# Expert stage: the down products as three split passes with the token rows moving

## The chip, the cores and the metric

One core of one Trainium2 chip runs the whole program. The metric is the device time of that core in microseconds (us); a run is one launch of the program, and the median of three runs is given. A profile is one more execution, with every instruction's start and duration. Engines: PE is TensorE (with PEld for its weight loads), DVE is VectorE, ACT is ScalarE, POOL is GpSimd, SP is SyncE.

## What is computed

Eight layers run one after the other on x of 128 x 64 tokens with 128 channels: four cross attentions with a feed-forward layer behind each. The change touches the third feed-forward layer alone, a mixture of 32 experts (64 hidden units each) and one shared expert (128 hidden units). From the reference:

```python
logits = jnp.einsum('th,eh->te', x, gate_w)
scores = jax.nn.sigmoid(logits)
...                                   # two of four groups of experts, then the best 8 of 32
topk_w = topk_w / (topk_w.sum(-1, keepdims=True) + 1e-20)
topk_w = topk_w * ROUTED_SCALING
...
g = jnp.einsum('th,eih->eti', x, expert_gate)
u = jnp.einsum('th,eih->eti', x, expert_up)
outs = jnp.einsum('eti,ehi->eth', jax.nn.silu(g) * u, expert_down)
...
final = (gathered * topk_w[:, :, None]).sum(1)
shared = _mlp(residuals, shared_gate, shared_up, shared_down)
return final.reshape(orig_shape) + shared
```

x goes in normalised, and the result is added to x times a gate. All is float32.

## The kernel before, and how its expert stage is built

The stage is the function `experts`. The 8192 tokens are 16 groups of 512 (4 tiles of 128). The hidden units of all experts are computed for every token, side by side: 2048 routed ones and 128 shared ones, cut into 17 **blocks** of 128 units (NB = 17, of which NR = 16 are routed). A block holds two experts. One block of one group, called m = 17 g + j, goes through the engines so:

- PE, `gate_up`: two products of weights (standing) with the group's 512 token columns (moving), each as three passes of `product3` (L354, L355, L356). An operand is split beforehand into a high and a low part of type fp32r, and high x high, high x low and low x high are summed in PSUM. So six matmuls of 512 columns. `ps_g` and `ps_u` have two PSUM banks each, so `gate_up` of block m waits for the multiplication of block m - 2 (`u_read`).
- ACT, `silu` (L1615): silu of the gate product, from PSUM.
- DVE, `mult` (L1662): silu times the up product (which is in PSUM) into `aT`, which has two buffers.
- DVE, `weight` (L1672): `aT` times the routing weights of the block's two experts, `wb`, both in SBUF. Block 16 is the shared expert and has none; there a tiny memset signals instead. `wb` is a row of the weights spread over 64 partitions by DMAs that SP issues (L1526), into a ring of 8 buffers (WR = 8).
- PE, `down` (L1581): four float32 matmuls with the 128 x 128 pieces of `aT` standing and the down weights moving, summed over the 17 blocks in one PSUM bank, `acc`. The trace shows each as two instructions.

At a group's end DVE adds `acc` times the gate to x (`added`, L1779), and the next group's first `down` waits for that. Between the blocks of group g the work for group g + 1 is placed by the number j in `body`: on PE the transposes of the normalised rows (j = 0), the router (j = 1), the turn of the weights (j = 11); on ACT the matching copies and the exponential of the router's sigmoid, which needs another activation table than silu; on DVE the split of hT (L343, L347; j = 1), 13 parts of routing arithmetic (two in each of j = 2 to 7, one in j = 8), the moments of group g + 2 (L302, L307; j = 9) and its scaling (L316, four instructions; j = 11). POOL does two small operations on 4 columns per group for the normalisation (L324, L326) and nothing else. Each engine runs its own list in the order of the code; `by_pairs` makes a loop over pairs of groups and writes the last pair out. In iteration j PE does `gate_up` of block j + 2, then `down` of block j; ACT does `silu` of j + 2, DVE `mult` and `weight` of j + 2, then the extra work of j.

Of the kernel before, what the change touches and what calls it, by code (L numbers as in the profile page):

```python
# [36 lines left out]
class Chip:  # L37
# [1432 lines left out]

def experts(c, d):


# [2 lines left out]
    V, A, T, G = nc.vector, nc.scalar, nc.tensor, nc.gpsimd  # L1478
    n = c.ngroup
    NB, NR = W2N // P, NE2 * I2 // P  # L1480
    WR = 8
    w = c.carve()
    hn = w([TG, P])
    hT = [w([GT]), w([GT])]
    r = c.carve(c.parts)
    hTh, hTl = [r([GT]), r([GT])], [r([GT]), r([GT])]
    wgh, wgl, wuh, wul = (r([W2N]) for _ in range(4))
    sg, aT = [w([GT]), w([GT])], [w([GT]), w([GT])]
    wT, wb = [w([GT]), w([GT])], [w([GT]) for _ in range(WR)]
    wts = [w([TG, NE2]), w([TG, NE2])]  # L1490
# [1 line left out]
    top, gt, eq = w([TG * 4, 8]), w([TG, 4, 4]), w([TG, 4, 4])  # L1492
    gs, rank, t8, ws = w([TG, 4]), w([TG, 4]), w([TG, 8]), w([TG])
    ps_g, ps_u = (tuple(c.ps[:, i + j, :] for j in range(2)) for i in (0, 2))
    acc, ps_x = c.ps[:, 6, :], c.ps[:, 7, :]
    norm = Norm(c, "f2_ln", hn)
    sem = lambda s: c.sem("f2_" + s)
    x_ready, x_out, gu_ready, silu_ready, u_read, a_ready, y_ready, added, link = (
        sem(s) for s in ("x", "x_out", "gu", "silu", "u_read", "a", "y", "added", "link"))
    down_done, wts_ready, norm_link = sem("down"), sem("wts"), sem("norm_link")  # L1500
    high_ready, low_ready, w_high, w_low = sem("high"), sem("low"), sem("w_high"), sem("w_low")
# [4 lines left out]
    def ahead(g, u, j, k=2):  # L1506

        return (g, u, j + k) if j + k < NB else (g + 1, 1 - u, j + k - NB)

    def at(g, u, j):  # L1510

# [2 lines left out]
    with nc.Block() as block:  # L1514
        @block.sync
        def _(sp):
            def spread(g, u):

                sp.wait_ge(x_out, g * 3 + 3)
                sp.dma_start(rows[u], wT[u][0:NE2, :]).then_inc(rows_in, 16)  # L1520
                sp.wait_ge(rows_in, g * 16 + 16)
                for j in range(NR):
                    if not (isinstance(g, int) and g == 0 and j < WR):
                        sp.wait_ge(a_ready, g * NB + (j - WR + 1) if j >= WR else g * NB + (j - WR))
                    for e in range(2):
# [9 lines left out]
            by_pairs(sp, n, body)  # L1535

        @block.gpsimd
        def _(pool):
            with pool.Fori(0, n) as g:
                norm.pool(pool, g)  # L1540

        @block.tensor
        def _(te):
# [45 lines left out]
            turn_weights(0, 0)  # L1589

            def body(g, u, last_pair):
# [12 lines left out]
            by_pairs(te, n, body)  # L1604

        @block.scalar
        def _(act):
# [19 lines left out]
            act.sem_inc(added, 1)  # L1627
# [3 lines left out]
            take_hT(0, 0), sigmoid_exp(0), silu(0, 0, 0), silu(0, 0, 1), take_weights(0, 0)  # L1631

            def body(g, u, last_pair):
                end = last_pair and u == 1
                for j in range(NB):
                    if not (end and j + 2 >= NB):
# [8 lines left out]
            by_pairs(act, n, body)  # L1645

        @block.vector
        def _(ve):
# [5 lines left out]
            def mult(g, u, j):  # L1654
                m, b = at(g, u, j)
                ve.wait_ge(silu_ready, m + 1)
                if not (isinstance(g, int) and g == 0 and j < 2):
                    if j < 2:
                        ve.wait_ge(y_ready, g) if j == 1 else ve.wait_ge(down_done, g * (NB - 1))
                    else:  # L1660
                        ve.wait_ge(down_done, g * (NB - 1) + (j - 1))
                out = V.tensor_tensor(aT[b], sg[b], ps_u[b], ALU.mult)  # L1662
                out.then_inc(u_read, 1)
                if j == NB - 1:
                    ve.wait_ge(u_read, m + 1)
                    V.memset(c.pause[:, 1:2], 0.0).then_inc(a_ready, 1)
# [96 lines left out]
            def body(g, u, last_pair):  # L1763
                end = last_pair and u == 1
                for j in range(NB):
                    if not (end and j + 2 >= NB):
                        block_of(*ahead(g, u, j))
                    if j == 1 and not end:
                        split(g + 1, 1 - u)
                    if 2 <= j < 9 and not end:  # L1770
# [3 lines left out]
                        norm.take_moments(ve, g + 2)  # L1774
                    if j == 11 and not last_pair:
                        norm.scale(ve, g + 2)
                ve.wait_ge(y_ready, g + 1)
# [4 lines left out]
            by_pairs(ve, n, body)  # L1782

# [398 lines left out]
def program(nc, d, layers=range(8)):  # L2182

    ctx = ExitStack()
    with ctx:
# [13 lines left out]
        c.close_work()  # L2199
        for layer in layers:  # L2200

            parts = {0: 4 * GT + 12 * P * 2 + 32 * D, 1: 4 * GT + 2 * NE0 * QKV, 2: 4 * GT + 12 * P * 2 + 32 * D, 5: 4 * GT + 4 * W2N, 6: 4 * GT + 12 * P * 2 + 64 * D}
            c.open_work({0: 17 * 1024, 2: 17 * 1024, 6: 13 * 1024, 1: 12 * 1024, 5: 12 * 1024}.get(layer, 26 * 1024), parts.get(layer, 0))
            if layer in (0, 2, 6):
                wide_attention(c, d, layer // 2)
            elif layer == 4:
# [95 lines left out]
```

## Time and profile before

| what | value |
| --- | --- |
| median of 3 runs | 3582.87 us (3581.49 to 3583.41) |
| profiled execution, own time | 3580.62 us |
| its span | 3578.5 us |
| mean granted TensorE clock | 0.959 of full speed |
| PE busy | 90% |
| DVE busy | 71% |
| ACT busy | 46% |
| POOL busy | 33% |
| expert stage | about 1929 to 2619 us of the span |
| its period per group | 41.5 us |

The profile has a page for the whole span and views on request: timelines of single instructions, groups of equal instructions by line, waits (who waited for whom), and windows with each engine's busy time. The period per group comes from line L1779, which runs once per group, from 1995.3 to 2617.8 us with 15 periods between. "Busy" says nothing of the gaps between instructions, some tens of ns each.

### The profile page before, as it was taken

The page shows a single profiled execution, that of the slowest core. Times are in us where ns is not written, and L with a number is a line of the kernel's source. Part 1 is how long each engine was busy: PE and PEld are TensorE (multiplying, and loading weights), DVE is VectorE, ACT ScalarE, POOL GpSimd, SP SyncE. Part 2 cuts the span into 40 slices and gives each one's busy share as a digit, 9 for nine tenths or more (in the row PEclk, how much of TensorE's full clock was granted, in tenths as well). Part 3 has the DMA queues.
Part 4 walks back from the last instruction along what each step waited for, and adds up shares of the span by engine and source line. Part 5 has one row for each costly group of instructions (what it writes and reads, how often), then busy time and mean ns, then how long its engine had stood idle before and what let it go on. Part 6 is the DMA issues. An engine that isn't in the chain of part 4 may idle for free. (4 is left out here: it accounts for less than half of the span.)

```text
span 3578.5 us, 78637 instructions
## 1 busy us (share of the span) xinstructions
PE 3205.1 (90%) x27370; PEld 2479.6 (69%) x27370; DVE 2528.8 (71%) x7156; ACT 1630.0 (46%) x3136; POOL 1170.3 (33%) x1359
## 2 busy tenths in 40 slices
PE   5999888888888999948997999999989999999978
PEld 3666577777777666645666888888866666666646
DVE  3666688888887555557777777777767777777732
ACT  2566433333333656516665333333245555555533
POOL 3555300000001555443441000000036566566532
PEclk9999989999999999958998999999999999999989
DMA  4000000000000000001111323333300000000001
GB/s 143 10 9 9 1 1 1 1 1 1 1 1 3 10 9 9 3 0 57 26 25 43 105 95 96 107 108 103 104 21 8 9 9 7 9 7 9 5 15 32
DMA packets 70603, 108.15 MB, mean 30 GB/s; under 512 B 13984, under 2 KB 24224, under 8 KB 69952
## 3 DMA queue, kind: packets, MB, share of 16 engines
q1 hardware_dynamic: 66048, 96.89, 8.7%
q10 hardware_dynamic: 4416, 9.59, 0.9%
q8 instruction: 65, 1.06, 0.1%
q14 instruction: 74, 0.61, 0.1%
HBM read 97.51 MB, written 5.24 MB: 29 GB/s over the span
## 5 line engine op out<-in xcount | busy, mean ns | idle before, releaser
L354 PE MATMUL ps<-parts 96*128 96x512 f32 (+2 forms) x2080 | 884.1, 425 | 22.0 <-DVE work L1662 7.4
L356 PE MATMUL ps<-parts 96*128 96x512 f32 (+2 forms) x2080 | 799.6, 384 | 0.0
L355 PE MATMUL ps<-parts 96*128 96x512 f32 (+2 forms) x2080 | 799.5, 384 | 0.0
L354 PEld LDWEIGHTS ps<-parts 96*128 96x128 f32 (+1 forms) x2080 | 402.5, 193 | 120.9 <-issue 47.1
L739 ACT ACTIVATE work<-ps 128x512 f32<-128x512 f32 x512 | 305.8, 597 | 394.5 <-PE ps L356 367.7
L324 POOL TENSOR_TENSOR rstd<-mv,eps 128x4 f32<-128x4 f32 x144 | 29.9, 208 | 1348.3 <-DVE mv L307 1348.2
L356 PEld LDWEIGHTS ps<-parts 96*128 96x128 f32 (+1 forms) x2080 | 400.3, 192 | 66.9
L355 PEld LDWEIGHTS ps<-parts 96*128 96x128 f32 (+1 forms) x2080 | 403.9, 194 | 44.7
L1615 ACT ACTIVATE work<-ps 128x512 f32<-128x512 f32 x272 | 163.0, 599 | 453.5 <-PE ps L356 453.4
L702 PEld LDWEIGHTS ps<-work 64*64 64x64 f32 x8192 | 221.6, 132 | 207.8 <-issue 207.8
L2095 DVE SCALAR_TENSOR_TENSOR work<-ps,work 128x192 f32<-128x192 f32 x896 | 323.8, 410 | 54.2 <-PE ps L356 41.9
L848 DVE TENSOR_REDUCE work<-work 128x8 f32<-128x512 f32 (+1 forms) x256 | 175.7, 686 | 231.9 <-ACT work L751 231.6
L523 POOL TENSOR_TENSOR work<-work 128x512 f32<-128x512 f32 x256 | 266.8, 1042 | 149.9 <-DVE work L850 148.4
L1581 PEld LDWEIGHTS ps<-early,work 128*128 128x128 f32 x2176 | 281.3, 191 | 29.7 <-DVE work L1672 11.3
L1581 PE MATMUL ps<-early,work 128*128 128x128 f32 x2176 | 289.0, 276 | 8.1 <-DVE x L1779 8.0
L702 PE MATMUL ps<-work 64*64 64x128 f32 x8192 | 282.6, 275 | 11.6 <-ACT work L792 11.6
L1662 DVE TENSOR_TENSOR work<-work,ps 128x512 f32<-128x512 f32 x272 | 185.8, 683 | 133.3 <-PE ps L1581 133.1
L832 DVE SCALAR_TENSOR_TENSOR ps<-ps,work 128x512 f32<-128x512 f32 x192 | 134.1, 698 | 135.7 <-PE ps L625 127.6
L835 DVE TENSOR_REDUCE work<-ps 128x8 f32<-128x512 f32 x256 | 176.9, 691 | 64.2 <-PE ps L625 57.6
L316 DVE TENSOR_SCALAR work<-x,mv,rstd 128x128 f32 (+1 forms) x456 | 174.7, 446 | 50.8 <-POOL rstd L326 50.8
L792 ACT ACTIVATE work<-ps 128x512 f32<-128x512 f32 x256 | 152.9, 597 | 112.1 <-PE ps L675 112.1
L1672 DVE TENSOR_TENSOR work<-work 128x512 f32<-128x512 f32 x256 | 177.1, 692 | 15.5 <-DMA work<-expert_rows 2.9
(283 smaller groups left out, 5700.4 us busy)
## 6 DMA issues: line engine op xcount, KB each, us to landing
work<-expert_rows SPq DMA_DIRECT2D x512, 128.0 KB, 2.9
work<-in_ctxT SPq DMA_DIRECT2D x72, 192.0 KB, 2.3
out<-x SPq DMA_DIRECT2D x16, 256.0 KB, 2.3
work<-work SPq DMA_DIRECT2D x224, 16.0 KB
early<-in_l0f_w ACTq DMA_DIRECT2D x1, 1536.0 KB, 15.3
early<-in_l2f_g SPq DMA_DIRECT2D x1, 1088.0 KB, 6.6
early<-in_l2f_u SPq DMA_DIRECT2D x1, 1088.0 KB, 8.8
early<-in_l2f_d SPq DMA_DIRECT2D x1, 1088.0 KB, 11.0
```

What stands on the lines that cost most here:

```text
L354: T.matmul(out, lh, rh, start=True, stop=False)
L355: T.matmul(out, lh, rl, start=False, stop=False)
L356: return T.matmul(out, ll, rh, start=False, stop=True)
L523: G.tensor_tensor(pn[t % 2], pr[t % 2][:, :, 0:S], bc(rec[t % 2], 2, S), ALU.mult).then_inc(p_ready, 1)
L702: pv = T.matmul(acc[p][half, t, :], ptT[t % 2][rows, j, half], vp[t % 2][rows, int(p != b), j, :], start=(un.p == 0 and j == 0 and (t == 0 ...
L739: A.activation(vp[t % 2][:, e, :, :].rearrange("p j c -> p (j c)"), ps_v[e], ACT.Copy).then_inc(v_done[e], 1)
L835: V.tensor_reduce(mx[t % 2], ps_s, AX.X, ALU.max).then_inc(max_ready, 1)
L848: V.tensor_reduce(den[t % 2], pr[t % 2], AX.X, ALU.add).then_inc(sum_ready, 1)
L1581: last = T.matmul(acc[:, t * D:(t + 1) * D], aT[b][:, t * P:(t + 1) * P], c.w["l2f_d"][:, j, :], start=(j == 0 and t == 0), stop=(j == NB ...
L1662: out = V.tensor_tensor(aT[b], sg[b], ps_u[b], ALU.mult)
L1672: V.tensor_tensor(aT[b], aT[b], wb[j % WR], ALU.mult).then_inc(a_ready, 1)
L2095: V.scalar_tensor_tensor(out=part_sum[t % 2][e], in0=z, scalar=r, in1=part_sum[t % 2][e], op0=ALU.mult, op1=ALU.add).then_inc(z_read, 1)
```

## The change

The down product gets the same form as gate and up: its weights `wd` stand, and the 512 token columns of `aT` move, in three passes of fp32r parts. The weights are split once at the start of the stage (high part by ACT, low part by POOL). `aT` is split in every block: ACT copies the high part to `ah` (`high_part`), POOL subtracts it from `aT` into `al` (`low_part`), both in rings of three (AR = 3); PE's `down` waits for `al_ready`. The second buffer of `aT` is freed by POOL's subtraction now: `mult` of block m waits for `al_ready` of block m - 2. The sum comes out with channels on the partitions, in one of two PSUM banks `ps_d`; ACT copies it to SBUF (`take_down`, `yT`) and PE turns it back with four transposes into `acc` (`turn_back`), three blocks into the next group; DVE adds it there (`add`, j = 3). `gate_up` and `silu` run three blocks ahead of `down` where they ran two; DVE stays at two. The ring `wb` shrinks from 8 to 4 buffers. The first pair of groups is now written out as well.

```diff
-    WR = 8
+    WR, AR = 4, 3
...
+    ps_d = tuple(c.ps[:, 4 + i, :] for i in range(2))
...
+            def low_part(g, u, j):
+
+                m, b = at(g, u, j)
+                pool.wait_ge(ah_ready, m + 1)
+                if not (isinstance(g, int) and g == 0 and j < AR):
+                    pool.wait_ge(down_done, downs_before(g, j))
+                pool.sem_inc(low_begun, 1)
+                G.tensor_tensor(al[j % AR], aT[b], ah[j % AR].bitcast(FP), ALU.subtract).then_inc(al_ready, 1)
+
+            norm.pool(pool, 0)
+            pool.wait_ge(wd_high, 1)
+            G.tensor_tensor(wdl.rearrange("p j c -> p (j c)"), c.w["l2f_d"].rearrange("p j c -> p (j c)"),
+                            wdh.bitcast(FP).rearrange("p j c -> p (j c)"), ALU.subtract).then_inc(wd_low, 1)
+            norm.pool(pool, 1)
+
+            def body(g, u, last_pair):
+                for j in range(NB):
+                    low_part(g, u, j)
+                    if j == 10 and not last_pair:
+                        norm.pool(pool, g + 2)
...
             def down(g, u, j):
                 m, b = at(g, u, j)
-                te.wait_ge(a_ready, m + 1)
+                te.wait_ge(al_ready, m + 1)
                 if j == 0:
-                    te.wait_ge(added, g + 1)
+                    need(te, yt_out, g - 1)
+                T.matmul(ps_d[u], wdh[:, j, :], ah[j % AR], start=(j == 0), stop=False)
+                T.matmul(ps_d[u], wdl[:, j, :], ah[j % AR], start=False, stop=False)
+                T.matmul(ps_d[u], wdh[:, j, :], al[j % AR], start=False, stop=(j == NB - 1)).then_inc(down_done, 1)
+
+            def turn_back(g):
+
+                te.wait_ge(yt_out, g + 1)
+                need(te, added, g)
                 for t in range(TG):
-                    last = T.matmul(acc[:, t * D:(t + 1) * D], aT[b][:, t * P:(t + 1) * P], c.w["l2f_d"][:, j, :],
-                                    start=(j == 0 and t == 0), stop=(j == NB - 1), skip_group_check=True)
-                last.then_inc(y_ready if j == NB - 1 else down_done, 1)
+                    last = T.transpose(acc[:, t * P:(t + 1) * P], yT[:, t * P:(t + 1) * P], c.w["ident"][:, :])
+                last.then_inc(y_ready, 1)
...
+            def high_part(g, u, j):
+
+                m, b = at(g, u, j)
+                act.wait_ge(a_ready, m + 1)
+                if not (isinstance(g, int) and g == 0 and j < AR):
+                    act.wait_ge(down_done, downs_before(g, j))
+                A.activation(ah[j % AR], aT[b], ACT.Copy).then_inc(ah_ready, 1)
+
+            def take_down(g, u):
+                act.wait_ge(down_done, g * NB + NB)
+                need(act, y_ready, g)
+                A.activation(yT, ps_d[u], ACT.Copy).then_inc(yt_out, 1)
...
-                    if not (end and j + 2 >= NB):
+                    if not (end and j + 1 >= NB):
+                        high_part(*ahead(g, u, j, 1))
+                    if not (end and j + LAG >= NB):
                         silu(*ahead(g, u, j))
+                    if j == 1 and not (isinstance(g, int) and g == 0):
+                        take_down(g - 1, 1 - u)
...
                 ve.wait_ge(silu_ready, m + 1)
                 if not (isinstance(g, int) and g == 0 and j < 2):
-                    if j < 2:
-                        ve.wait_ge(y_ready, g) if j == 1 else ve.wait_ge(down_done, g * (NB - 1))
-                    else:
-                        ve.wait_ge(down_done, g * (NB - 1) + (j - 1))
+                    ve.wait_ge(al_ready, m - 1)
                 out = V.tensor_tensor(aT[b], sg[b], ps_u[b], ALU.mult)
...
+                    if j == 3 and not (isinstance(g, int) and g == 0):
+                        add(g - 1)
```

**POOL's list**, before, for the whole stage (a loop of two instructions per group, L324 and L326 in `norm.pool`):

```order
L1539 UNCONDITIONAL_BRANCH
L1539 ISA
L324 TENSOR_TENSOR rstd<-mv,eps 128x4
L326 TENSOR_TENSOR rstd<-rstd,half 128x4
L1539 REGISTER_ALU
L1539 COMPARE_AND_BRANCH
```

And of the change, the stage's start with the first two groups (L1575 the low part of the down weights, L1571 `low_part`):

```order
L324 TENSOR_TENSOR rstd<-mv,eps 128x4
L326 TENSOR_TENSOR rstd<-rstd,half 128x4
L1575 TENSOR_TENSOR parts<-early,parts 128x2176
L324 TENSOR_TENSOR rstd<-mv,eps 128x4
L326 TENSOR_TENSOR rstd<-rstd,half 128x4
L1571 TENSOR_TENSOR parts<-work,parts 128x512 x11
L324 TENSOR_TENSOR rstd<-mv,eps 128x4
L326 TENSOR_TENSOR rstd<-rstd,half 128x4
L1571 TENSOR_TENSOR parts<-work,parts 128x512 x17
```

POOL now has 17 subtractions of 512 columns per group, and the normalisation's two operations stand behind the eleventh of them.

**DVE's list** in the loop, before, at a group's end (L1662 `mult`, L1672 `weight`, L1779 the addition to x):

```order
L1662 TENSOR_TENSOR work<-work,ps 128x512
L1672 TENSOR_TENSOR work<-work 128x512
L1779 ISA
L1779 SCALAR_TENSOR_TENSOR x<-ps,tg,x 128x512
L1656 REGISTER_ALU
L1662 TENSOR_TENSOR work<-work,ps 128x512
```

And of the change, in iteration j = 3, behind `mult` and `weight` of block 5 (L1766 to L1775 routing parts 2 and 3, L1856 the addition, L1735 `mult` of block 6):

```order
L1763 REGISTER_ALU
L1764 MEMSET pause 1x1
L1766 MAX work<-work 128x8 x16
L1728 REGISTER_ALU
L1769 TENSOR_TENSOR work<-work 128x16
L1772 REGISTER_ALU
L1774 TENSOR_TENSOR work<-work 128x64
L1775 TENSOR_TENSOR work<-work 128x64
L1856 ISA
L1856 SCALAR_TENSOR_TENSOR x<-ps,tg,x 128x512
L1732 REGISTER_ALU
L1735 TENSOR_TENSOR work<-work,ps 128x512
```

The addition moved from a gap between groups to the iteration with the longest routing part.

## Rows read from the trace of the kernel before

**Rows 1.** The page, part 1: busy time, share of the span, instructions.

```profile
PE 3205.1 (90%) x27370; PEld 2479.6 (69%) x27370; DVE 2528.8 (71%) x7156; ACT 1630.0 (46%) x3136; POOL 1170.3 (33%) x1359
```

**Rows 2.** Window of one group: PE, PEld, DVE, ACT, POOL busy; PEclk; DMA.

```profile
2037.50:2079.00 41.50, 40.72 (x253) 35.84 (x252) 32.20 (x99) 13.70 (x22) 1.21 (x2) 1.00 0.32 103
```

**Rows 3.** Waits, 1995 to 2500 us: us in total, times, longest.

```profile
ACT work L1615 <- PE ps L356: 336.0, 193, 2.4
DVE work L1662 <- PE ps L1581: 94.9, 84, 1.8
...
PEld ps L354 <- DVE work L1662: 7.5, 24, 0.5
PE ps L1581 <- DVE x L1779: 6.6, 13, 0.5
```

**Rows 4.** Timeline of one block: start us, us, engine, line, operation.

```profile
2103.04 0.48 PE L354 MATMUL ps<-parts 128*128 128x512 f32 x1
...
2103.35 0.40 PE L355 MATMUL ps<-parts 128*128 128x512 f32 x1
...
2104.49 1.05 PE L1581 MATMUL ps<-early,work 128*128 128x128 f32 x8
...
2105.30 0.48 PE L354 MATMUL ps<-parts 128*128 128x512 f32 x1
```

**Rows 5.** Groups by form, 2000 to 2500 us: busy us, mean ns, idle before.

```profile
L1662 DVE TENSOR_TENSOR work<-work,ps 128x512 f32<-128x512 f32 x203 | 138.6, 683 | 93.7 <-PE ps L1581 93.5
L1672 DVE TENSOR_TENSOR work<-work 128x512 f32<-128x512 f32 x191 | 132.2, 692 | 9.9 <-DVE work L1662 0.6
L1615 ACT ACTIVATE work<-ps 128x512 f32<-128x512 f32 x203 | 121.6, 599 | 332.1 <-PE ps L356 331.9
...
L1615 ACT ACT_TABLE_LOAD x12 | 15.4, 1283 | 0.2
...
L316 DVE TENSOR_SCALAR work<-x,mv,rstd 128x128 f32 x48 | 13.3, 341 | 0.0
...
L302 DVE BATCH_NORM_STATS2 st<-x 128x6 f32 x48 | 10.4, 279 | 0.0
...
L347 DVE TENSOR_TENSOR parts<-work,parts 128x512 fp32r<-128x512 f32 x12 | 8.3, 692 | 0.4
```

**Rows 6.** Timeline, start of the stage.

```profile
1928.78 2.02 ACT L1629 ACTIVATE parts<-early 128x2176 fp32r<-128x2176 f32 x1 [2.37 <-PEq L2217]
...
1938.20 0.22 DVE L1683 TENSOR_SCALAR work<-work 128x128 f32<-128x128 f32 x1
...
1938.99 0.63 PE L355 MATMUL ps<-parts 128*128 128x512 f32 x1
...
1939.42 0.63 PE L356 MATMUL ps<-parts 128*128 128x512 f32 x1
...
1945.80 0.29 DVE L1743 TENSOR_TENSOR work<-work 128x128 f32<-128x128 f32 x1
```

**Rows 7.** By line, whole span: duration ns min/median/max.

```profile
L505 POOL TENSOR_TENSOR parts<-work,parts x58: 1285/1304/1316, 80.9 to 3365.5; 96x512 fp32r<-96x512 f32 x58
L840 DVE TENSOR_TENSOR work<-work x128: 166/169/1209, 2640.7 to 3408.5; 128x8 f32<-128x8 f32 x128
L843 DVE TENSOR_TENSOR work<-ps,work x256: 678/688/692, 67.5 to 3408.8; 128x512 f32<-128x512 f32 x128
L513 POOL TENSOR_TENSOR parts<-parts,zero x128: 1260/1279/1327, 55.3 to 3378.6; 96x512 fp32r<-96x512 f32 x128
```

**Rows 8.** Timeline of the wide-head attention, POOL and DVE.

```profile
2677.91 1.29 POOL L503 TENSOR_TENSOR parts<-work,zero 96x512 fp32r<-96x512 f32 x1
2678.02 1.21 DVE L840 TENSOR_TENSOR work<-work 128x8 f32<-128x8 f32 x1
```

**Rows 9.** Window of the gated stage; columns as in rows 2.

```profile
600.00:800.00 200.00, 166.91 (x1036) 151.89 (x1036) 162.85 (x556) 62.35 (x185) 10.95 (x21) 0.91 0.00 1
```

More of the change, by code:

```diff
@@ L1469, in _, with by_two_groups, both @@
             by_pairs(ve, n, body)
+def by_two_groups(eng, n, body):
+    def both(it, last):
+        for u in range(2):
+            body(it * 2 + u, u, last)
+    by_twos(eng, n // 2, both)
 def experts(c, d):
@@ L1487, in experts @@
     wgh, wgl, wuh, wul = (r([W2N]) for _ in range(4))
+    wdh, wdl = (r([NB, D]) for _ in range(2))
+    ah, al = [r([GT]) for _ in range(AR)], [r([GT]) for _ in range(AR)]
+    yT = w([GT])
     sg, aT = [w([GT]), w([GT])], [w([GT]), w([GT])]
@@ L1500, in experts @@
     down_done, wts_ready, norm_link = sem("down"), sem("wts"), sem("norm_link")
+    low_begun = sem("low_begun")
+    ah_ready, al_ready, yt_ready, yt_out, wd_high, wd_low = (sem(s) for s in ("ah", "al", "yt", "yt_out", "wd_high", "wd_low"))
+    LAG = 3
     high_ready, low_ready, w_high, w_low = sem("high"), sem("low"), sem("w_high"), sem("w_low")
@@ L1504, in experts, with ahead, behind, downs_before @@
     LINKS = 16
-    def ahead(g, u, j, k=2):
+    def ahead(g, u, j, k=LAG):
         return (g, u, j + k) if j + k < NB else (g + 1, 1 - u, j + k - NB)
+    def behind(g, u, j, k):
+        return (g, u, j - k) if j >= k else (g - 1, 1 - u, j - k + NB)
+    def downs_before(g, j):
+        last = j - AR if j >= AR else {0: NB - 2, 1: NB - 1, 2: NB - 3}[j] - NB
+        return g * NB + last + 1
     def at(g, u, j):
@@ L1533, in body @@
                     spread(g + 1, 1 - u)
-            by_pairs(sp, n, body)
+            by_two_groups(sp, n, body)
         @block.gpsimd
         def _(pool):
-            with pool.Fori(0, n) as g:
-                norm.pool(pool, g)
+            def low_part(g, u, j):
[15 more added lines that the diff above has]
+                        norm.pool(pool, g + 2)
+            by_two_groups(pool, n, body)
         @block.tensor
@@ L1589, in _ @@
             turn_weights(0, 0)
+            gate_up(0, 0, 2)
+            te.wait_ge(wd_low, 1)
             def body(g, u, last_pair):
@@ L1602, in body @@
                     down(g, u, j)
-            by_pairs(te, n, body)
+                    if j == 2 and not (isinstance(g, int) and g == 0):
+                        turn_back(g - 1)
+            by_two_groups(te, n, body)
+            turn_back(n - 1)
         @block.scalar
@@ L1630, in _ @@
             A.activation(wuh, c.w["l2f_u"], ACT.Copy).then_inc(w_high, 1)
-            take_hT(0, 0), sigmoid_exp(0), silu(0, 0, 0), silu(0, 0, 1), take_weights(0, 0)
+            take_hT(0, 0), sigmoid_exp(0)
+            A.activation(wdh.rearrange("p j c -> p (j c)"), c.w["l2f_d"].rearrange("p j c -> p (j c)"), ACT.Copy).then_inc(wd_high, 1)
+            silu(0, 0, 0), silu(0, 0, 1), take_weights(0, 0), high_part(0, 0, 0), silu(0, 0, 2)
             def body(g, u, last_pair):
@@ L1635, in body @@
                 for j in range(NB):
-                    if not (end and j + 2 >= NB):
+                    if not (end and j + 1 >= NB):
+                        high_part(*ahead(g, u, j, 1))
+                    if not (end and j + LAG >= NB):
                         silu(*ahead(g, u, j))
+                    if j == 1 and not (isinstance(g, int) and g == 0):
+                        take_down(g - 1, 1 - u)
                     if j == 0 and not end:
@@ L1643, in body @@
                         take_weights(g + 1, 1 - u)
-            by_pairs(act, n, body)
+            by_two_groups(act, n, body)
+            take_down(n - 1, 1)
         @block.vector
@@ L1766, in body @@
                     if not (end and j + 2 >= NB):
-                        block_of(*ahead(g, u, j))
+                        block_of(*ahead(g, u, j, 2))
                     if j == 1 and not end:
@@ L1776, in body, with add @@
                         norm.scale(ve, g + 2)
+                    if j == 3 and not (isinstance(g, int) and g == 0):
+                        add(g - 1)
+            def add(g):
                 ve.wait_ge(y_ready, g + 1)
@@ L1780, in body @@
                                        op0=ALU.mult, op1=ALU.add).then_inc(added, 1)
-            by_pairs(ve, n, body)
+            by_two_groups(ve, n, body)
+            add(n - 1)
 def gated_attention(c, d):
@@ L2200, in program @@
         for layer in layers:
-            parts = {0: 4 * GT + 12 * P * 2 + 32 * D, 1: 4 * GT + 2 * NE0 * QKV, 2: 4 * GT + 12 * P * 2 + 32 * D, 5: 4 * GT + 4 * W2N, 6: 4 * GT + 12 * P * 2 + 64 * D}
-            c.open_work({0: 17 * 1024, 2: 17 * 1024, 6: 13 * 1024, 1: 12 * 1024, 5: 12 * 1024}.get(layer, 26 * 1024), parts.get(layer, 0))
+            parts = {0: 4 * GT + 12 * P * 2 + 32 * D, 1: 4 * GT + 2 * NE0 * QKV, 2: 4 * GT + 12 * P * 2 + 32 * D, 5: 10 * GT + 6 * W2N, 6: 4 * GT + 12 * P * 2 + 64 * D}
+            c.open_work({0: 17 * 1024, 2: 17 * 1024, 6: 13 * 1024, 1: 12 * 1024, 5: 8704}.get(layer, 26 * 1024), parts.get(layer, 0))
             if layer in (0, 2, 6):
```

1 line of the change is left out of this document (removed).

## The prediction

> **What bounds the kernel now.** I read the page's busy shares first: PE is busy 90% of the span, DVE 71% [rows 1]. The change touches one stage, so the next view is a window of one group there: of 41.5 us PE is busy 40.72, DVE 32.20, ACT 13.70, POOL 1.21, with the clock granted in full [rows 2]. The waits say who waits for whom [rows 3]: ACT and DVE wait for PE (336.0 and 94.9 us of 500), while PE waits for DVE 7.5 us at a gate product and 6.6 us at a down product, the latter once per group at the addition to x. So PE sets the pace. But DVE is close behind. Its 99 instructions have 30 to 40 ns between them (`mult` of 0.683 us and `weight` of 0.692 us [rows 5] take about 0.71 and 0.70 us of its list each), so it is occupied 32.2 + 99 x 0.035 = 35.7 us of the 41.5.
>
> **PE: what is removed and added.** A block takes 2105.30 - 2103.04 = 2.26 us [rows 4]. The five gate and up passes from 2103.35 to 2104.49 are 0.228 us apart, and the down product takes the 0.81 us from there, plus some 0.08 that the first pass behind it loses (0.31 us to the second one, not 0.228). With nine passes a block is 9 x 0.228 = 2.05 us: 0.21 us less. Per group that is 17 x 0.21 = 3.6 us; the wait for the addition, 6.6 / 13 = 0.5 us, goes too; the four transposes of `turn_back` cost 0.5 us. PE alone would need 17 x 2.05 = 34.9 us for blocks and about 2.3 us for transposes, router and turns: 37.2 us per group. If PE stayed the bound, 41.5 - 37.2 = 4.3 us per group would be gained.
>
> **DVE: not less work, and a new neighbour.** DVE's 35.7 us stay, so it has only 1.5 us per group to spare against 37.2, 0.09 us per block. What the change adds beside it is POOL's subtraction, 17 times per group. Its duration is that of L505, the same operation with the same kinds of operands on 96 partitions: 1.30 us [rows 7]. What such an operation does to DVE the attention stages show. L840 reads two SBUF tensors of 8 columns and takes 0.169 us at the median, but up to 1.209 us [rows 7]. In the timeline it starts at 2678.02, 0.11 us behind a POOL operation that runs from 2677.91 to 2679.20, and ends at 2679.23 [rows 8]. So it waited for POOL's operation to within about 0.15 us of its end, a hold of about 1.15 us. L843, of the same kind but with one operand in PSUM, never exceeds 0.692 us in 256 instances [rows 7]. Hence `mult` (one operand in PSUM) can run beside the subtraction; `weight`, `split`'s L347 and the TENSOR_TENSOR parts of the routing can't start during it.
>
> The Trainium skill ("SBUF — State Buffer", section "SBUF: two separate sides") states this as a rule: DVE and GpSimd share one pair of SBUF ports, as an exclusive lock for a whole instruction, and a DVE instruction takes it with two SBUF inputs or in a two-port mode. The rows agree for DVE waiting. By the page POOL also waits for `weight`, which no row here shows; in the walk below that alone would make a pair of plain blocks 4.55 us instead of 4.0, some 8 us over the stage.
>
> **A walk through DVE's list.** Let `weight` of block m end at 0. ACT's `high_part` needs about 0.62 us (as silu's 0.599 [rows 5]) and a handover of 0.04 us; with 0.09 us to POOL the subtraction starts at 0.75 and holds until 1.90.
> - A plain block: `mult` of m + 1 runs 0 to 0.71. `weight` is ready at 0.72, just about when POOL starts. If POOL wins, `weight` runs 1.90 to 2.60: a period of 2.60 us that repeats itself. If `weight` wins, `mult` of m + 2 must wait for the subtraction, since it frees `aT`: end of the subtraction at 2.05 if POOL runs beside `weight`, 2.7 if it is held back, and every second period is the blocked one; two blocks take 4.0 or 4.55 us. So 2.0 to 2.6; I take 2.4, since the order is a near tie in which L840 shows that 0.11 us behind POOL is too late. Four periods per group are plain: 9.6.
> - Block 16 without `weight` and block 0 behind it: 3.9 us for the two.
> - Behind `split` (0.42 + 0.69 us [rows 5]): POOL is held to 1.14, then `weight` of the next block waits until 2.3: 3.0.
> - The seven iterations with routing: the 13 parts last 1945.80 + 0.29 - 1938.20 = 7.9 us [rows 6], 1.13 per iteration. With 1.13, then `mult`, `weight` is ready at 1.84 and goes at 1.90: 2.6. Where a part with two SBUF operands falls into 0.75 to 1.90, it waits, and `mult` and `weight` follow: 3.3. I take 3.0 (both occur), 21.0, plus 0.78 for the addition that now stands in iteration 3: 21.8.
> - The exponential: two table loads of 1.283 us [rows 5] stand before `high_part` of block 3 and `silu` of block 5 on ACT and delay POOL's subtraction of block 3 by about 1.2 us: 1.0.
> - Moments (four L302 of 0.279 us [rows 5] and what follows, 1.3 us): 2.7. POOL does the normalisation's two operations (1.3 us) in front of the subtraction of block 11, which frees `aT` for `mult` of block 13: 3.2. Scaling, four L316 [rows 5] in 1.1 us: 2.95.
>
> Sum: 9.6 + 3.9 + 3.0 + 21.8 + 1.0 + 2.7 + 3.2 + 2.95 = 48.2 us per group, 6.7 more than 41.5. PE follows: its `gate_up` waits for `mult`. Expressed per subtraction, (48.2 - 35.7) / 17 = 0.74 us of each hold of 1.15 shows on DVE. 15 groups give 100 us; the last, without extra work, about 2.
>
> **Both ends of the stage.** At the start ACT copies the down weights (2.02 us as L1629 [rows 6], ahead of silu but beside PE's first products: nothing) and POOL subtracts 2176 columns, 5 us (1.30 x 2176 / 512 = 5.5 at most). Routing starts at 1938.20 and its first TENSOR_TENSOR meets that hold: + 4 us, since PE's third block waits for DVE's first `mult`. At the end the last block goes through `high_part`, the subtraction, `take_down` and `turn_back` before it is added: 0.7 + 1.4 + 0.65 + 0.5 against nothing, + 3 us with the shorter product. The ring of 4 `wb` costs nothing: a buffer is refilled four blocks ahead, 8 us or more, and SP's list isn't longer; this cover would go only if DVE ran at 2.05 us per block and the DMAs took over 6.
>
> Sum: 100 + 2 + 4 + 3 = + 109 us on 3580.6, the profiled execution's own time, so 3690; the median lies 2.3 us higher: **3692**.
>
> **Rivals.**
> A. *PE stays the bound* (faster). The POOL holds fall into DVE's `mult`s and free routing parts. 15.5 x (41.5 - 37.2) = 67 us off, 7 us for the ends, some 5 us for peaks of DVE's list: 3528. It needs a visible hold under 0.09 us per subtraction. For it: ACT and POOL are nearly idle, and `mult` alone covers 0.71 of 1.15. Against it: `mult`'s place in the list is not where the subtraction falls. 7%.
> B. *No holds, but DVE peaks stop PE* (no change). Iterations 3 to 6 load DVE with 4.2, 2.4, 3.0 and 2.4 us against PE's 2.05, and PE's slack is 2 x 2.05 - 1.37 - 0.65 - 0.71 = 1.4 us (two blocks less product, silu, `mult`). PE would lose about 4 us per group: 41.2, so 3580.6 - 5 + 7 + 2.3 = 3585. The break-even with before is a visible hold of (41.5 - 35.7) / 17 = 0.34 us. 5% for within 0.2%, 5% more for a gain short of A.
> C. *The walk with mild holds or with all of them.* Plain blocks 2.0 and routing ones 2.6: 43 us, 3618. Plain 2.6 and routing 3.3: 52.5 us, 3760. These are ends of the forecast, not cases beside it.
> D. *The clock falls* because PE waits 20% of the time. The gated stage, PE busy 83%, was granted 0.91 [rows 9]; at the lower of the two levels (1.2 GHz) a pass takes 1939.42 - 1938.99 = 0.43 us [rows 6], and a block 9 x 0.43 = 3.9 us. The whole stage at it would take 67 us per group: + 400 us, about 3990. A tenth of it there hides behind DVE. 3%.
>
> **The numbers.** Forecast with its ends (C) 80%, A 7%, B 10%, D 3%. Median 3692; the range, 3580 to 3765, reaches to B (about half of which lies in it) and leaves out A and D. A measurement can tell about 0.2% (7 us) from no change. Faster by over 0.2%: A and half of B, 12%. Within: 5%. Slower: 83%.
>
> **What would show it.** In the trace of the changed kernel `mult` stays at 0.69 us, while `weight` has a median well over 0.7 and a maximum near 1.8; single routing TENSOR_TENSORs reach 1.3 us; POOL is busy some 22 us per group; the group's period is 48 us; PE waits at L354 for DVE, and ACT less for PE. I am wrong if `weight` stays at 0.69 us beside the subtraction; if the period is PE's 37 us; or if the records show long waits for the DMAs of `wb` or a granted clock well under 0.9.

## The result, and the profile after

| | before | after |
| --- | --- | --- |
| median | 3582.18 us (3580.63 to 3583.41, 4 runs) | 3644.47 us (3643.76 to 3646.29, 4 runs) |
| ratio, 95% interval | | 1.0175 [1.0157, 1.0193] |
| span of the profiled execution | 3578.5 us | 3642.1 us |
| mean granted TensorE clock | 0.959 | 0.953 |

The kernel became slower by 1.75%, 62 us. The page, part 1, of the kernel after, to be set beside [rows 1]:

```profile
PE 3200.8 (88%) x26074; PEld 2389.7 (66%) x26074; DVE 2644.8 (73%) x7156; ACT 1801.1 (49%) x3425; POOL 1547.9 (42%) x1632
```

PE has 1296 instructions fewer, as intended, though its busy time (it counts overlapping records) fell by only 4 us and that of its loads by 90; POOL's busy time grew by 378 us. DVE's grew by 116 us with the same 7156 instructions: time inside its records, not more of them. The window of one group says the same, beside [rows 2] (columns in its first line):

```profile
core 0: us, PE busy (x) PEld busy (x) DVE busy (x) ACT busy (x) POOL busy (x), PEclk, DMA share, GB/s
2137.44:2183.16 45.72, 40.24 (x175) 29.69 (x174) 39.93 (x100) 24.54 (x41) 24.47 (x19) 1.00 0.29 94
```

DVE is busy 39.93 us of a group where it was busy 32.20 in the 41.50 us of [rows 2] (32.58 in a full period of 41.90). And the period grew. The first `mult` of two consecutive groups, before (L1662) and after (L1735), from the timelines of DVE (start us, us, engine, line):

```profile
2117.44 0.69 DVE L1662 TENSOR_TENSOR work<-work,ps 128x512 f32<-128x512 f32 x1 [1.46 <-PE ps L1581]
...
2159.34 0.69 DVE L1662 TENSOR_TENSOR work<-work,ps 128x512 f32<-128x512 f32 x1 [1.53 <-PE ps L1581]
```

```profile
2137.44 0.69 DVE L1735 TENSOR_TENSOR work<-work,ps 128x512 f32<-128x512 f32 x1 [0.38 <-POOL parts L1571]
...
2183.16 0.69 DVE L1735 TENSOR_TENSOR work<-work,ps 128x512 f32<-128x512 f32 x1 [0.37 <-POOL parts L1571]
```

That is 41.90 and 45.72 us. (41.5, which the prediction used, was an average that contained the shorter last group.) The waits from 2000 to 2500 us, beside [rows 3] (us in total, times, longest):

```profile
POOL parts L1571 <- ACT parts L1690: 217.8, 134, 3.3
...
PEld ps L354 <- DVE work L1735: 90.2, 107, 2.7
ACT work L1672 <- PE ps L356: 63.6, 115, 1.6
PE ps L354 <- DVE work L1735: 50.7, 39, 2.2
DVE work L1735 <- POOL parts L1571: 44.2, 43, 1.4
```

Before, the load of the first gate pass waited 7.5 us for DVE; now it waits 90.2 and the pass itself 50.7 us (they overlap). ACT waited 336.0 us for PE, now 63.6. DVE waited for PE and now waits for POOL. PE is no longer the bound. The groups by form in the same stretch (busy us, mean ns, idle before), beside [rows 5]:

```profile
L1571 POOL TENSOR_TENSOR parts<-work,parts 128x512 fp32r<-128x512 f32 x185 | 253.5, 1375 | 228.7 <-ACT parts L1690 217.8 <-PE ps L1627 10.2
...
L1745 DVE TENSOR_TENSOR work<-work 128x512 f32<-128x512 f32 x175 | 160.1, 915 | 10.6 <-DVE work L1735 1.4
...
L1735 DVE TENSOR_TENSOR work<-work,ps 128x512 f32<-128x512 f32 x186 | 126.5, 680 | 44.9 <-POOL parts L1571 44.2 <-issue 0.2
...
L343 DVE CAST parts<-work 128x512 fp32r<-128x512 f32 x11 | 16.6, 1507 | 0.0
...
L1760 DVE TENSOR_TENSOR work<-work,l2f_bias 128x128 f32<-128x128 f32 x11 | 13.8, 1252 | 0.4
```

`weight` (L1745) takes 0.915 us on average, not 0.692, while `mult` (L1735) stays at 0.680. The cast of `split` and the first TENSOR_TENSOR of the routing take 1.51 and 1.25 us, where they took 0.42 and 0.29. The holds are not spread over all instances; by line (duration ns min/median/max):

```profile
L1745 DVE TENSOR_TENSOR work<-work x256: 691/693/1806, 1957.3 to 2672.3; 128x512 f32<-128x512 f32 x128
```

113 of the 256 are held, those that start while a subtraction runs; the median is unchanged. Two places in the timeline show one hold in each direction:

```profile
2213.34 1.28 POOL L1571 TENSOR_TENSOR parts<-work,parts 128x512 fp32r<-128x512 f32 x1 [1.42 <-ACT parts L1690]
2213.69 1.48 DVE L1745 TENSOR_TENSOR work<-work 128x512 f32<-128x512 f32 x1
...
2216.01 0.69 DVE L1745 TENSOR_TENSOR work<-work 128x512 f32<-128x512 f32 x1
...
2216.04 1.81 POOL L1571 TENSOR_TENSOR parts<-work,parts 128x512 fp32r<-128x512 f32 x1 [1.41 <-ACT parts L1690]
```

At 2213.69 `weight` starts 0.35 us behind POOL's subtraction, is held until about 0.15 us before its end (2214.62) and then needs its 0.69. At 2216.01 it starts 0.03 us ahead of POOL, runs in 0.69, and POOL's record is 1.81 us long, 0.52 more than its 1.29. So the hold works both ways, as the Trainium skill has it ("SBUF — State Buffer", section "SBUF: two separate sides"); its second half, which no row of before could show, is in this row.

The granted clock is not quite as before either. Before, it stays at its upper level from 1960 to 2620 us; after, it falls briefly to the lower one in ten of fifteen groups, for instance at 2204 us, behind two waits of PE for DVE of 1.75 and 2.22 us (columns as above):

```profile
2183.16:2228.88 45.72, 41.14 (x175) 31.00 (x174) 39.97 (x99) 24.63 (x41) 24.48 (x19) 0.96 0.28 93
```

This group, granted 0.96, takes the same 45.72 us as the one above with 1.00: in this kernel the dips cost nothing, since DVE and POOL set the pace.

### The profile page after: what moved, and what is told of

Same layout as the page of the kernel before. It is cut to its first block and busy times, and to the rows that moved or that the text cites. A ratio compares the mean times of both kernels' runs of the same rounds, so it can differ in the third digit from the quotient of the medians.

```text
span 3642.1 us, 77197 instructions
## 1 busy us (share of the span) xinstructions
PE 3200.8 (88%) x26074; PEld 2389.7 (66%) x26074; DVE 2644.8 (73%) x7156; ACT 1801.1 (49%) x3425; POOL 1547.9 (42%) x1632
## 5 line engine op out<-in xcount | busy, mean ns | idle before, releaser
L1571 POOL TENSOR_TENSOR parts<-work,parts 128x512 fp32r<-128x512 f32 x272 | 373.7, 1379 | 329.8 <-ACT parts L1690 314.4
L324 POOL TENSOR_TENSOR rstd<-mv,eps 128x4 f32<-128x4 f32 x144 | 30.0, 208 | 696.5 <-DVE mv L307 694.7
L1690 ACT ACTIVATE parts<-work 128x512 fp32r<-128x512 f32 x272 | 171.7, 631 | 236.5 <-DVE work L1745 229.9
L1745 DVE TENSOR_TENSOR work<-work 128x512 f32<-128x512 f32 x256 | 234.0, 914 | 17.3 <-DMA work<-expert_rows 2.9
L1735 DVE TENSOR_TENSOR work<-work,ps 128x512 f32<-128x512 f32 x272 | 185.0, 680 | 73.9 <-POOL parts L1571 72.6
L316 DVE TENSOR_SCALAR work<-x,mv,rstd 128x128 f32 (+1 forms) x456 | 175.8, 447 | 50.8 <-POOL rstd L326 50.8
L1672 ACT ACTIVATE work<-ps 128x512 f32<-128x512 f32 x272 | 161.9, 595 | 102.6 <-PE ps L356 101.1
```

What stands on the lines that cost most here:

```text
L316: last = V.tensor_scalar(self.hn[:, t, :], src, c.mv[:, t, 0:1], c.rstd[:, t:t + 1], ALU.subtract, ALU.mult)
L1571: G.tensor_tensor(al[j % AR], aT[b], ah[j % AR].bitcast(FP), ALU.subtract).then_inc(al_ready, 1)
L1745: V.tensor_tensor(aT[b], aT[b], wb[j % WR], ALU.mult).then_inc(a_ready, 1)
```

## Experiments

Theory **H**: the time is POOL's hold on DVE's instructions with two SBUF operands or in a two-port mode, and DVE's on POOL. (By the latter the cast and the TENSOR_SCALARs with one SBUF tensor are meant; no record names the mode.) Rival **L**: it is the longer way of a block through ACT and POOL before `aT` is free. Rival **P**: it is the peaks of DVE's list, which PE's shorter blocks no longer cover. Group periods below are distances between the first `mult` of consecutive groups in the middle of the stage. Ratios are against runs of the kernel before on the same chip.

**e1: POOL's subtraction cut to 8 columns**, but for the first three blocks. Most of the low part is then stale; the number of instructions and all waits stay.

```diff
+                cols = slice(0, GT if isinstance(g, int) and g == 0 and j < AR else 8)
-                G.tensor_tensor(al[j % AR], aT[b], ah[j % AR].bitcast(FP), ALU.subtract).then_inc(al_ready, 1)
+                G.tensor_tensor(al[j % AR][:, cols], aT[b][:, cols], ah[j % AR][:, cols].bitcast(FP), ALU.subtract).then_inc(al_ready, 1)
```

> The changed kernel, with POOL's subtraction of each block cut from 512 to 8 columns (but for the first three blocks of the stage); this leaves most of the low parts of aT stale, all waits and all of PE's, ACT's and DVE's work stay. Theory H (POOL's hold on DVE's two-SBUF-operand instructions costs the time): weight (L1745) back to 0.69 us in nearly every instance, group period from 45.7 to about 41 us, 3580 us in all. Rival L (the longer way of a block through ACT and POOL before aT is free, not the hold): the same, since 1.1 us of that way go too. Rival P (the peaks of DVE's list with PE's shorter blocks): little changes, over 3625 us.

Measured: 3559.37 us, ratio 0.9948 [0.9928, 0.9968], period 40.0 us. The subtraction's size accounts for the whole loss and more: without it the change is a gain. It doesn't tell H from L. Its waits, in the same stretch:

```profile
DVE work L1736 <- ACT work L1673: 57.8, 85, 1.3
PEld ps L354 <- DVE work L1736: 46.5, 65, 1.8
...
DVE work L1736 <- POOL parts L1572: 3.1, 13, 0.3
```

DVE now waits for silu and no longer for POOL; PE still waits 46.5 us for DVE.

**e2: a third buffer for `aT`** (in a part of `early` that is free).

```diff
-    sg, aT = [w([GT]), w([GT])], [w([GT]), w([GT])]
+    sg, aT = [w([GT]), w([GT])], [w([GT]), w([GT]), c.early[:, 3 * W2N:3 * W2N + GT]]
...
-                if not (isinstance(g, int) and g == 0 and j < 2):
-                    ve.wait_ge(al_ready, m - 1)
-                out = V.tensor_tensor(aT[b], sg[b], ps_u[b], ALU.mult)
+                if not (isinstance(g, int) and g == 0 and j < AR):
+                    ve.wait_ge(al_ready, downs_before(g, j))
+                out = V.tensor_tensor(aT[j % AR], sg[b], ps_u[b], ALU.mult)
```

> The changed kernel with a third buffer for aT, so that mult of a block waits for the subtraction three blocks back and not two. H: the waits of mult for POOL (72.6 us in the changed kernel) go, but weight and the routing parts stay held; only the plain blocks gain, from 2.18 to about 2.05 us, 3625 us. L: the way of a block no longer counts, 41 us per group, 3585 us. P: unchanged, 3644 us.

Measured: 3641.75 us, ratio 1.0173 [1.0154, 1.0192], period 45.1 to 45.9 us. The idle time of `mult` for POOL fell from 72.6 us to 20.4, that for silu rose from 0.3 to 27.8 (what ended it: us, times):

```profile
  ACT work L1672: 27.8, 70
  POOL parts L1571: 20.4, 15
```

and the time hardly moved. L falls: it expected 41 us per group. H had expected some 20 us, which didn't come either. In part what DVE no longer waits it spends being held: `weight` takes 0.979 and 0.919 us on average in its two places of writing, not 0.915, and silu is waited for instead. In part it is the clock, as two consecutive groups show (columns as above, granted clock third from the end):

```profile
2186.71:2231.87 45.16, 40.36 (x175) 31.06 (x174) 40.65 (x99) 23.96 (x41) 24.88 (x19) 0.96 0.29 95
2231.87:2277.51 45.64, 40.98 (x175) 32.18 (x174) 41.17 (x100) 23.97 (x41) 25.08 (x19) 0.93 0.29 94
```

Every group of e2 has one dip to the lower level or two, and those with two take 0.5 to 0.7 us longer. If the first dip costs as much as the second, the third buffer alone would give about 44.6 us per group; that is an estimate from these periods, since no group of e2 is without a dip. Even so it is 1.1 of the 5.7 us that e1 took away.

**e3: the two products of a block in another order and place.** silu stays in PSUM; `weight` comes first and reads it there, `mult` then reads the up product there. Each has one SBUF operand. The results are the same. Three things move besides the operands: only `mult`, now the second, writes `aT` and waits for the subtraction; the PSUM banks are released one product later (`gate_up` waits for `a_ready`, not `u_read`); and block 16 loses its tiny memset.

```diff
-                    te.wait_ge(u_read, m - 1)
+                    te.wait_ge(a_ready, m - 1)
...
-                A.activation(sg[b], ps_g[b], ACT.Silu).then_inc(silu_ready, 1)
+                A.activation(ps_g[b] if j < NR else sg[b], ps_g[b], ACT.Silu).then_inc(silu_ready, 1)
...
-                out = V.tensor_tensor(aT[b], sg[b], ps_u[b], ALU.mult)
-                V.tensor_tensor(aT[b], aT[b], wb[j % WR], ALU.mult).then_inc(a_ready, 1)
+                V.tensor_tensor(sg[b], ps_g[b], wb[j % WR], ALU.mult).then_inc(weighted, 1)
...
+                V.tensor_tensor(aT[b], sg[b], ps_u[b], ALU.mult).then_inc(a_ready, 1)
```

> The changed kernel with DVE's two products of a block in the other order and from other places: ACT leaves silu in PSUM, weight multiplies it there by wb into sg, mult then multiplies sg by the up product in PSUM. The same number of instructions and the same results, but neither instruction has two SBUF operands. H: both stay at 0.69 us beside the subtraction, POOL's records go to 1.30 us; the splits and the routing parts are still held, some 3 us per group; period 41 to 43 us, 3585 to 3600 us. L: the order and the wait on aT are as before, 3640 us. P: unchanged, 3644 us.

Measured: 3591.43 us, ratio 1.003 [1.0018, 1.0042], period 41.8 to 41.9 us in groups granted the full clock and 42.3 to 42.6 in those with a dip. `weight` (L1735 here; duration ns min/median/max) never exceeds 0.694 us:

```profile
L1735 DVE TENSOR_TENSOR work<-ps,work x256: 656/691/694, 1948.5 to 2609.6; 128x512 f32<-128x512 f32 x128
```

and POOL's subtraction (L1572) is back at 1.290 us, while the cast, still in a two-port mode, is held as before (groups by form, 2000 to 2500 us):

```profile
L1572 POOL TENSOR_TENSOR parts<-work,parts 128x512 fp32r<-128x512 f32 x203 | 261.4, 1290 | 218.0 <-ACT parts L1691 212.9 <-PE ps L1628 5.0
...
L343 DVE CAST parts<-work 128x512 fp32r<-128x512 f32 x11 | 15.6, 1420 | 0.0
```

3.6 of 45.7 us per group went, and with them every hold on `weight`: as H has it, and neither L (3640 us) nor P (3644 us). The wait on `aT` that now stands one product later can have a part in it, but by e2, where it was moved by a whole block, no more than about 1.1 us. The later release of the PSUM banks can only cost.

**e4 and e8: the hold by itself, in the kernel before.** One POOL instruction per block, released by the same signal as the down product, whose result nobody uses or waits for; e4 subtracts 512 columns of zeros, e8 writes 1280 columns and reads nothing. In both, POOL's normalisation of group g + 2 stands behind the instruction of block 10, as in the change.

```diff
+            def beside(g, j):
+                pool.wait_ge(a_ready, g * NB + j + 1)
...
+                G.tensor_tensor(scratch, c.zero[:, 0:GT], c.zero[:, 0:GT], ALU.subtract).then_inc(beside_done, 1)
```

> The kernel before, with one subtraction of 128x512 zeros on POOL per block, released by the same signal as the down product (a_ready), whose result nobody uses or waits for. H: DVE's weight is held to 1.2 us and more in part of its instances; DVE's 35.7 us of 41.9 per group grow by 17 times up to 0.5, so the period goes to 43 to 44 us and the time to 3600 to 3620 us. L and P: nobody waits for POOL, 3582 us.

> As e4_beside, but POOL's instruction per block is a memset of 1280 columns: about as long (some 1.2 us), but it reads nothing from SBUF. If the hold needs a POOL instruction that reads SBUF, as the Trainium skill's page on SBUF has it for DVE instructions with two SBUF operands: weight stays at 0.69 us, the two-port instructions (L316, L343) may still be held, 3582 to 3590 us. If any POOL instruction holds them: as e4, 3620 us.

Measured: e4 3625.37 us, ratio 1.0129 [1.0108, 1.0151], period 44.6 to 44.9 us; e8 3579.88 us, ratio 0.9999 [0.9988, 1.0011], period 41.9 us. In e4 `weight` (L1687) reaches 1.565 us, and a routing part that begins 0.16 us behind POOL's instruction takes 1.03 us, not 0.28. By line, by form (L347, the low part of hT, two SBUF operands) and from the timeline:

```profile
L1687 DVE TENSOR_TENSOR work<-work x256: 691/692/1565, 1953.5 to 2657.4; 128x512 f32<-128x512 f32 x128
```

```profile
L347 DVE TENSOR_TENSOR parts<-work,parts 128x512 fp32r<-128x512 f32 x12 | 16.9, 1410 | 0.4
```

```profile
2199.57 1.04 POOL L1545 TENSOR_TENSOR work<-zero 128x512 f32<-128x512 f32 x1 [1.87 <-DVE work L1687]
2199.73 1.03 DVE L1746 TENSOR_TENSOR work<-work 128x128 f32<-128x128 f32 x1
```

In e8, by line and by form (L1688 `weight`, L1546 the memset):

```profile
L1688 DVE TENSOR_TENSOR work<-work x256: 691/692/695, 1949.4 to 2611.4; 128x512 f32<-128x512 f32 x128
```

```profile
L1546 POOL MEMSET work<- 128x1280 f32 x204 | 239.5, 1174 | 231.0 <-DVE work L1688 221.7 <-DVE pause L1682 5.9
...
L316 DVE TENSOR_SCALAR work<-x,mv,rstd 128x128 f32 x48 | 22.4, 797 | 0.0
...
L1756 DVE TENSOR_SCALAR work<-work 128x4 f32<-128x4 f32 x12 | 12.5, 1043 | 0.4
...
L347 DVE TENSOR_TENSOR parts<-work,parts 128x512 fp32r<-128x512 f32 x12 | 8.3, 692 | 0.4
```

POOL's memset is longer (1.174 us) than e4's subtraction (1.04 us), and neither `weight` nor L347 takes longer than before. They do meet: in e8 44 of the 256 `weight`s and all 15 L347 behind 1940 us start while a memset runs, and each takes its 0.69 us; in e4 36 and 15 start while a subtraction runs, and all are held. But L316 and L1756, which read one SBUF tensor, are held in e8 too: 0.797 us on average, not 0.341 [rows 5], and 1.043, not 0.17. Both kinds are named by the Trainium skill ("SBUF — State Buffer", section "SBUF: two separate sides"), and the two runs bear them out: two SBUF operands meet a POOL instruction that reads, two-port instructions met one that only writes as well. e8's holds are few and cost nothing that shows in the period. e4 also says that 45 us of loss need no new wait at all, since nobody waits for POOL's instruction there; nor is it the place of the normalisation, which e8 shares, nor the clock, which stays at its upper level in the loop of both.

**e5: the low part of the down weights later.**

```diff
-            pool.wait_ge(wd_high, 1)
...
             norm.pool(pool, 1)
+            pool.wait_ge(norm.ready, 2)
+            pool.wait_ge(wd_high, 1)
```

> The changed kernel with one edit at the start: POOL's subtraction of the 2176 columns of down weights runs after the second group's normalisation and so after all of the first group's routing. H: the 4.18 us that L1760 takes there go back to 0.29 us, the first mult moves from 1953.7 to about 1949.7 us, 4 us less, 3640 us. If the hold there were hidden behind PE: no change. The subtraction may now meet the first weight or the scaling, which would give up to 1 us back.

Measured: 3641.07 us, ratio 1.0179 [1.0157, 1.02], against 1.0175 of the change. In the timeline the routing's L1761 is back at 0.29 us and the subtraction meets the first `weight` instead:

```profile
1938.51 0.29 DVE L1761 TENSOR_TENSOR work<-work,l2f_bias 128x128 f32<-128x128 f32 x1
...
1948.95 4.80 POOL L1577 TENSOR_TENSOR parts<-early,parts 128x2176 fp32r<-128x2176 f32 x1 [1.23 <-DVE work L316]
...
1952.01 2.29 DVE L1746 TENSOR_TENSOR work<-work 128x512 f32<-128x512 f32 x1 [2.55 <-DMA work<-expert_rows]
```

That gives back 1.6 us there. The trace shows both holds; in the time neither the 4 us expected nor any other gain can be told.

**e6: the addition to x in iteration 14.** `if j == 3` becomes `if j == 14` on DVE.

> The changed kernel with the addition to x in iteration 14 and not 3 of DVE's list. P (peaks of DVE's list stop PE) and H agree that 0.74 us leave the period of the busiest stretch; what matters is whether iteration 14 can take it. P: some 0.7 us per group, 3633 us. If POOL and DVE alternate at the same pace whatever stands between (pure H): 0 to 0.3 us, 3640 us or more.

Measured: 3631.64 us, ratio 1.0147 [1.0126, 1.0167], period 45.1 us, 0.6 less. That is P's forecast (3633 us), not pure H's (3640 or more). So P is a part of it, beside H: iteration 3 was a peak, iteration 14 had room.

**e7: a version from both.** e3 with e5, e6, the high part of hT made by ACT from PSUM, `take_down` and `turn_back` one iteration later, and POOL's normalisation behind block 11.

> e3_psum_silu (neither product of a block with two SBUF operands) with the edits of e5 and e6, the high part of hT made by ACT from PSUM and not by DVE, POOL's normalisation one block later, and take_down and turn_back one iteration later. H and P together: from e3's 41.9 to 42.3 us per group the held cast (1.4 us) and the addition (0.7 us) leave the peaks, 40 to 40.5 us, and 4 us go at the start: 3555 to 3565 us, faster than the kernel before by 0.4 to 0.7%. H alone: 3585 us.

Measured: 3561.79 us over 6 runs, ratio 0.9957 [0.9941, 0.9973], period 40.9 us: faster than both kernels. Window of one group, columns as above:

```profile
2137.00:2178.00 41.00, 38.82 (x176) 30.39 (x175) 35.23 (x98) 24.25 (x41) 23.33 (x20) 1.00 0.33 105
```

DVE is busy 35.23 us, 3 more than before, POOL 23.33.

**e9 and e10: what is left.** e9 is e7 with e1's cut to 8 columns, e10 is e7 with the routing parts dealt out more evenly.

```diff
-                        for part in range(2 * j - 4, min(2 * j - 2, 13)):
+                        for part in ((0, 1), (2,), (3, 4), (5, 6), (7, 8), (9, 10), (11, 12))[j - 2]:
```

> e7_combined with POOL's subtraction cut to 8 columns as in e1 (most low parts of aT stale). H: what is still held there (L347, the routing parts with two SBUF operands) and the 1.1 us of a block's way go; e1 had 40.0 us per group with the addition still in iteration 3 and the cast on DVE, so 39 us, 3535 to 3545 us. If e7's 40.9 us are all set by DVE's peaks and the loop of gate product, silu and product, not by holds: 40.5 us or more, 3555 us.

> e7_combined with the routing parts dealt out more evenly: part 2 (16 maxima, 1.3 us) alone in iteration 3, the following parts two by two behind it, 11 and 12 in iteration 8. P: the peak of iteration 3 shrinks by 0.4 us, of which up to 0.4 us per group come off the time, 3555 to 3562 us. H: no change, 3562 us.

Measured: e9 3549.14 us, ratio 0.9923 [0.9904, 0.9942], period 39.6 us; e10 3563.5 us, ratio 0.9959 [0.9944, 0.9975], period 40.4 to 40.6 us. So 1.3 us per group are left in e7 for POOL's subtraction, holds and a block's longer way together, and 39.6 - 37.2 = 2.4 us are lost with no hold of note (37.2 being the prediction's estimate for PE alone). e10 takes 0.3 us off the period in the trace and nothing that the runs can tell. e9's waits:

```profile
DVE work L1738 <- ACT ps L1676: 64.6, 111, 1.0
PEld ps L354 <- DVE work L1748: 40.4, 78, 1.1
```

DVE waits for silu and PE for DVE. That fits the loop from gate product over silu and DVE's two products to the next product in the same PSUM bank, and it fits the crowded iterations; no run separates the two.

## Why the prediction was right, and where it was not

Direction and mechanism came as forecast. The size was + 62 us where the forecast was + 109, inside the range: nearly all of the difference lies in the period of a group, + 3.8 us where the walk had + 6.7.

**PE's own saving.** There is one: e1, without POOL's holds, has a period of 40.0 us against 41.9. Its size, 4.3 us, is not shown; no run reached the 37.2 us that PE alone was to need, the nearest is e9 with 39.6. The prediction's terms don't agree with each other either: 3.6 and 0.5 us off and 0.5 on are 3.6, which would leave 37.9.

**The hold.** 1.15 us of hold per subtraction, `mult` free, `weight` and routing parts held: all as in the rows after. The walk gave holds only to instructions with two SBUF operands; the cast of `split` (1.51 us, not 0.42) and the routing's first TENSOR_SCALAR (1.31, not 0.22) are held as well. And one sign was wrong: the median of `weight` was to be well over 0.7, and is 0.693; its maximum, 1.806, came as forecast. In the middle of the stage the 5.7 us between e1's 40.0 and 45.7 are the holds' share (with 1.1 us of each block's way, which by e2 can account for some 1.1 us of a group at most). Balance per group, with 37.2 for PE taken as given: 41.9, less 4.7 for PE, plus 2.8 that DVE's peaks and silu take back, plus 5.7 for holds, is 45.7.

**The walk.** It said 48.2 us, the trace has 45.7. Distances between the ends of consecutive `weight`s, beside the walk's: behind `split` 3.58 (3.0); the seven routing periods with the exponential 4.82, 4.57, 2.71, 2.90, 2.71, 2.70, 1.53, in sum 21.9 (22.8); moments, normalisation and scaling 8.4 (8.85); blocks 16 and 0 4.8 (3.9); the four plain ones 1.32, 1.32, 3.04, 1.32, in sum 7.0 (9.6). The plain blocks are the term that was mis-sized. The timeline shows them (POOL's row holds two subtractions):

```profile
2231.86 0.69 DVE L1745 TENSOR_TENSOR work<-work 128x512 f32<-128x512 f32 x1
...
2232.23 2.82 POOL L1571 TENSOR_TENSOR parts<-work,parts 128x512 fp32r<-128x512 f32 x2 [1.54 <-ACT parts L1690]
...
2233.74 0.69 DVE L1735 TENSOR_TENSOR work<-work,ps 128x512 f32<-128x512 f32 x1 [1.19 <-POOL parts L1571]
...
2234.58 1.01 DVE L1745 TENSOR_TENSOR work<-work 128x512 f32<-128x512 f32 x1 [0.16 <-DVE work L1735]
...
2235.51 0.67 DVE L1735 TENSOR_TENSOR work<-work,ps 128x512 f32<-128x512 f32 x1
...
2236.22 0.69 DVE L1745 TENSOR_TENSOR work<-work 128x512 f32<-128x512 f32 x1
```

There is no near tie: the walk had `weight` ready 0.72 us behind the `weight` before and POOL 0.75, and the trace has 0.63 and 0.87 at the least (here `weight` at 2231.86, POOL at 2232.23). So a plain block behind a held `weight` is free, and plain blocks are never held twice in a row: the pattern of 4.0 or 4.55 us per two blocks, which came out at 1.32 + 3.04 = 4.36, and not the mean with 2.60. Three of the four plain ones are the free half of a pair; of their held halves one is the 3.04, one is block 0 (in the 4.8 with block 16) and one stands behind the scaling. And the step on DVE's occupancy was wrong: from `mult` at 2235.51 to the end of `weight` at 2236.91, less the overlap of 0.08 with the `weight` before, are 1.32 us, not 1.41, because `weight`'s record and its successor's overlap. With it DVE is occupied some 34 us per group rather than 35.7. The periods of the walk were also compared with 41.5 and not with 41.9. The ends of the forecast (C) don't follow from its terms: 2.0 and 2.6 give 43.7 us per group, not 43, and 2.6 and 3.3 give 51.0, not 52.5.

**Both ends.** The start was right to 0.1 us: the first `mult` moved from 1949.7 to 1953.7, for the reason given,

```profile
1938.75 4.84 POOL L1575 TENSOR_TENSOR parts<-early,parts 128x2176 fp32r<-128x2176 f32 x1 [7.23 <-ACT parts L1701]
...
1939.56 4.18 DVE L1760 TENSOR_TENSOR work<-work,l2f_bias 128x128 f32<-128x128 f32 x1
```

and the tail, from the last `mult` to the end of the addition, grew from 2.8 to 6.1 us (+ 3). The last group, without extra work, was forecast 2 us longer and is 2.6 shorter: plain blocks again. Sum by the traces: 4.0 + 57.1 for 15 groups - 2.6 + 3.3 = 61.8 in the stage, of 63.6 of span.

**The rivals.** A failed: PE isn't the bound in any version of the change. B, no holds but peaks, is nearly e1, with 40.0 us per group where B has 41.2. D came only as short dips, 0.98 on average from 1960 to 2680 us where it was 1.00 before, and cost nothing in the changed kernel; in e2 and e3 they cost about 0.5 us per dip.

## What to carry to other kernels

An idle POOL isn't free capacity beside a busy DVE: count its SBUF-reading instructions as time of DVE too, unless DVE's instructions beside them have one operand in PSUM. Where a chain of elementwise products passes through PSUM anyway, choose the order in which each product reads one operand there; in e3 that was worth 53 us. Before reading a difference of a few us between two runs, compare the granted clock of single groups. Taking 0.2 us of every block from the bound engine brings only what the next one has to spare, in its worst stretch and not on average.

## What the runs showed of the hardware

A POOL instruction that only writes holds DVE's TENSOR_SCALAR from SBUF to SBUF (e8: 0.797 us for 0.341) but not those with two SBUF operands (0.692 throughout); one that reads SBUF holds the latter for nearly its length (e4: 1.410 us for 0.692). DVE's products with one operand in PSUM run beside it (e3: 0.694 us at most). Whoever comes second by as little as 0.03 us waits. That a third buffer for `aT` gained almost nothing although it took away most of DVE's waits for POOL had not been expected either: the two engines still exclude each other, and the waits were in part only its shape. The granted clock dipped to its lower level in ten of fifteen groups of the changed kernel and in every group of e2, where one dip more meant some 0.5 us more; the kernel before, with PE busy 646 of 660 us, had none between 1960 and 2620 us. PE waits for DVE in these versions, from 2000 to 2500 us for 2.2 us at the longest in the change and 3.3 in e2; e1 and e7, where the longest are 1.4 and 1.7 us, have no dip from 2000 us on. No run was made to test this.
